# Perceiver block on one core: the value product with two heads' columns as weights, and key blocks in column groups of their own

## Chip, cores and metric
One Trainium2 chip, one core. The metric is the device time of one execution in microseconds, the median over several runs.

## What is computed
A block of three parts, each with a layer norm ahead and a residual: cross attention of 128 rows to a context of 2048 rows, self attention with rotary embedding and a distance bias, and a mixture of 16 experts with the top 4 weighted. Batch 2, width 128, 16 heads of 8. The change touches the cross attention:

```
Qh = _split_heads(Q @ Wq.T + bq)
Kh = _split_heads(K @ Wk.T + bk)
Vh = _split_heads(V @ Wv.T + bv)
scores = jnp.einsum('bhqd,bhkd->bhqk', Qh, Kh) / scale
scores = scores - jnp.max(scores, axis=-1, keepdims=True)
attn = jax.nn.softmax(scores, axis=-1)
attn = jnp.clip(attn, EPS, None)
attn = attn / jnp.sum(attn, axis=-1, keepdims=True)
ctx = jnp.einsum('bhqk,bhkd->bhqd', attn, Vh)
```

## The kernel before
Each engine's program is written out by hand and synchronised with semaphores.

**Ahead.** Keys and values are projected from the context (`keys`, `vals`), keys are split into three bf16 parts whose sum is the fp32 key, and are stacked in `kst` for each pair of heads. The values lie in `vau` as [128 keys, block, head, 9]: eight columns and a column of ones, so that the same product gives the sum of the exponentials.

**The steps.** The cross attention runs in 64 steps (`TILES`), step t for batch t // 32, a group of four heads (t % 32) // 8 and two key blocks of 128. TensorE's order in a step, set by the loop at L1495:
- `scores(t)`, L1252: 8 products, which fill two PSUM banks of [128 keys, 512] (half a has heads a and a + 2 of the group for both blocks). The banks rotate among three (`EBANK`), so a score bank is free when ScalarE's exponential of three jobs before has read it (`bank_free`).
- now and then `turn` (L1233): the row maxima of the next head group are put into the queries' rows, once in eight steps; and small jobs of the first batch's way to the self attention (`SMALL_AT`), among them `sums_out` in step 34.
- `unit(t + 12)`, L1214: queries times keys for the maxima, 1024 columns in two banks, up to step 51. VectorE reduces it (`maxima`, L597).
- `values(t - 1)`, L1271: the value product, below.

ScalarE takes the exponentials (L1030), two of 512 columns per step, into four buffers `ex`. At step 32 it copies the accumulator bank 7 to `oS` (L1042) and `values(32)` waits for that.

**The value product before.** For each block i and head j of the group, weights are the 9 columns of `vau` and the moving operand is 128 columns of exponentials. The output of head j lies at partitions 32j to 32j + 8 of bank 7, so the four heads use four column groups of the array side by side, and a head group has 128 columns of the bank; a batch fills it with its four head groups. All 16 key blocks accumulate in place. In the trace each fp32 product is two hardware passes: 8 products are 16.

**Sums.** `sums_out` turns `oS` with four transposes (`turn_sums`, L1337) into PSUM, [128 queries, 4 groups, 4 heads, 32], of which `sums_in` (L624) and `normalise` (L618, L619) on VectorE read the sums and the values. For batch 0 this is in step 34, for batch 1 at L1585, after the last step: there TensorE's queue goes on with `norms` (L1096), `turn_normed2` (L1444), `sums_out(1)`, `logits_fixed` (L1528, L1529) and the experts' up projections (L1520), whose results ScalarE takes through GELU (L1052), after a table load.

**Beside the path.** GpSimd issues the loads of the constants (L469) and builds the position table `alibi` (L476), between pieces of the maxima (`max_terms`, L413 to L416) for which `turn` waits. The branch `clip_moves`/`clip_sums` is a slow way for rows that need the clip; with these inputs it isn't entered.

Of the kernel before, what the change touches and what calls it, by code (L numbers as in the profile page):

```python
# [25 lines left out]
B, S, D, H = 2, 128, 128, 16  # L26
DK = D // H
# [3 lines left out]
NK = CTX // 128  # L31
PAIRS = H // 2
GH = 4
NG = H // GH
# [16 lines left out]
def build(nc, x, ctxT, wq, wk, wv, wo, bias, bo, qkvw, projw, projb, slopes,  # L51
# [4 lines left out]
    with ExitStack() as es:  # L56
# [3 lines left out]
        def sem(name):  # L60
# [11 lines left out]
        sumrow = sb("sumrow", [128, GH])  # L72
# [30 lines left out]
        oS = sb("oS", [128, B, 512])  # L103
# [22 lines left out]
        fo = sb("fo", [128, 128])  # L126
# [36 lines left out]
        fe, fC = kr[:, 0, 0:512], kr[:, 0, 512:1024]  # L163

# [25 lines left out]
            "oS", "oT", "bnd", "cnt", "flag", "cn", "cnT", "cnTc", "o")}  # L190
# [69 lines left out]
        oS_v = oS[:].rearrange("p b n -> p (b n)")  # L260

# [9 lines left out]
        def clip_moves(sp, b):  # L271

            with sp.Fori(0, NG) as n:
                for r in range(2):
                    for a in range(2):
                        half = slice(HALF * a, HALF * a + HALF)
                        sp.dma_start(fq[half, r, a, :], qst[half, bass.ds(2 * n + r, 1), b * S:(b + 1) * S]
                                     .rearrange("p r n -> p (r n)")).then_inc(d_fg[b], 16)
                sp.dma_start(fo[:], oS[:, b, bass.ds(128 * n, 128)]).then_inc(d_fg[b], 16)
# [6 lines left out]
                sp.dma_start(oS[:, b, bass.ds(128 * n, 128)], facc[:]).then_inc(d_fs[b], 16)  # L286
            sp.wait_ge(d_fs[b], NG * 16)
            sp.wait_ge(f_end[b], 1)
# [223 lines left out]
        def _(dve):  # L512
# [100 lines left out]
            def normalise(b, bank):  # L613

                r = b % B
                o = ps[:, bank, :].rearrange("p (n g c) -> p n g c", n=NG, g=GH)
                r4 = rec[:, r, :].rearrange("p (n g) -> p n g", n=NG)
                link(dve.reciprocal(r4, o[:, :, :, DK]))  # L618
                dve.tensor_tensor(cn[:, r, :].rearrange("p (n g d) -> p n g d", n=NG, g=GH), o[:, :, :, 0:DK],  # L619
                                  r4.unsqueeze(3).broadcast_to([128, NG, GH, DK]), ALU.mult).then_inc(s["cn"], 1)  # L620

            def sums_in(b, bank):
                dve.wait_ge(s["oT"], 2 * b + 1)
                link(dve.tensor_copy(sumq[:, b, :].rearrange("p (n g) -> p n g", n=NG),  # L624
                                     ps[:, bank, :].rearrange("p (n g c) -> p n g c", n=NG, g=GH)[:, :, :, DK]))
# [100 lines left out]
            def normalise2(b):  # L726
                dve.wait_ge(s["oT"], 2 * b + 2)
                normalise(b, SELF[NG * b + 1])
# [10 lines left out]
            def small(kind, bank):  # L739

                if kind == "sums":
                    sums_in(0, bank)
                    normalise(0, bank)
# [86 lines left out]
            normalise(1, SUMS_B)  # L830
# [56 lines left out]
            with dve.If(bad_rows(dve)):  # L887
                dve.wait_ge(d_x, 2 * 16)
                link(dve.tensor_tensor(xs[:], xs[:], boB[:].unsqueeze(1).broadcast_to([128, B, D]), ALU.add))
                for b in range(B, 2 * B):  # L890
# [5 lines left out]
                    normalise(b, SUMS_B)  # L896
# [25 lines left out]
        def _(act):  # L922
# [110 lines left out]
            for t in range(TILES):  # L1033
# [50 lines left out]
        def _(pe):  # L1084
# [174 lines left out]
            def values(t):  # L1259
# [90 lines left out]
            def clip_sums(b):  # L1350
# [3 lines left out]
                with pe.Fori(0, NG) as n:  # L1354
                    pe.wait_ge(d_fg[b], (n + 1) * 80)
                    for j in range(GH):
                        last = pe.matmul(ps[:, CLIP_C, 128 * j:128 * j + 128], sumrow[:, j:j + 1].broadcast_to([128, 128]),
                                         fo[:], start=True, stop=True)
                    last.then_inc(f_C[b], 1)
                    with pe.Fori(0, NK) as c:  # L1360
# [8 lines left out]
                        for j in range(GH):  # L1369
                            last = pe.matmul(ps[32 * j:32 * j + DK + 1, CLIP_PV, 0:128], fv[:, j, :], fe[:, 128 * j:128 * j + 128],  # L1370
# [4 lines left out]
                turn_sums(oS[:, b], SUMS_B).then_inc(f_end[b], 1)  # L1375
# [305 lines left out]

def pick_tables():
# [11 lines left out]
def shape_tables():  # L1694
# [11 lines left out]
    sumrow = np.zeros((128, GH), np.float32)  # L1706
    sumrow[32 * np.arange(GH) + DK, np.arange(GH)] = 1
# [35 lines left out]
```

## Time and profile before

| | us |
|---|---|
| runs before | 215.56, 219.44, 219.81 (median 219.44) |
| the profiled execution | 215.47 |
| its span, first to last instruction | 213.7 |
| TensorE busy in the span | 190.7 (89%) |
| VectorE, ScalarE, GpSimd busy | 146.4, 149.1, 76.0 |
| mean granted TensorE clock | 0.999 of full |

The profile is of one execution. Times of rows are microseconds from the span's start. PE is TensorE's matmul, PEld its weight load, DVE VectorE, ACT ScalarE, POOL GpSimd. An arrow in brackets names what ended the idle time before a row. The steps of the cross attention lie between 39 and 130 us.

### The profile page before, as it was taken

Reading aid. Unit: us, or ns where it says so; the run is one execution under the profiler, and the core shown is the slowest. Engines: PE = TensorE matmul, PEld = TensorE weight load, DVE = VectorE, ACT = ScalarE, POOL = GpSimd, SP = SyncE. Lnnn points to the kernel's source line nnn. Section 1 sums busy time; section 2 is a strip of 40 time slices with the busy share of each in tenths; the row PEclk is TensorE's granted clock in tenths of the full one; section 3 lists DMA queues with packets and bytes.
Section 4 is the critical chain, followed back from the end, with each engine's and each line's share of the span. In section 5 each row is a group of like instructions: output and inputs, shape, how many; then the busy total and the mean of one; then the engine's idle time right before and its main releaser. Section 6 shows DMA issues by size and latency. Waiting matters only on the chain.

```text
span 213.7 us, 6350 instructions
## 1 busy us (share of the span) xinstructions
PE 190.7 (89%) x2551; PEld 131.4 (61%) x2551; DVE 146.4 (69%) x263; ACT 149.1 (70%) x331; POOL 76.0 (36%) x111
## 2 busy tenths in 40 slices
PE   4799899699999989979899999799889999999691
PEld 1345436355555545435454667697769998999681
DVE  5286499999999988988999846746983447212120
ACT  4677684589999988857798972977664645367760
POOL 6123689989889970110200001510000114090000
PEclk9999999999999999999999999999999999999999
DMA  6935332237347322257787712300000000000000
GB/s 115 303 123 216 115 94 92 90 100 272 104 112 200 106 88 83 95 164 213 213 325 231 232 38 77 123 2 0 3 0 3 0 0 15 0 2 3 0 0 25
DMA packets 8690, 21.26 MB, mean 100 GB/s; under 512 B 1664, under 2 KB 2784, under 8 KB 8656
## 3 DMA queue, kind: packets, MB, share of 16 engines
q1 hardware_dynamic: 7344, 19.47, 28.7%
q0 software_dynamic: 592, 0.74, 1.5%
q10 hardware_dynamic: 720, 0.59, 0.8%
q8 instruction: 22, 0.36, 0.7%
q14 instruction: 12, 0.10, 0.1%
HBM read 17.52 MB, written 3.28 MB: 97 GB/s over the span
## 4 chain that ended last, share of the span: by engine, by line
PE 67%; DVE 14%; ACT 8%; issue 3%; DMA 3%; POOL 2%; ACTq 1%; DVEq 0%
PE ps L1271 14%; PE ps L1520 12%; PE ps L1252 10%; PE ps L1553 9%; PE ps L1214 6%; DVE mx L597 5%; PE ps L1119 4%; DMA wks<-in_wk 3%; PE ps L1126 2%; ACT cT L1052 2%; PE ps L1138 2%; PE ps L1411 2%; POOL wr L495 1%; DVE sm L708 1%; ACT ex L1030 1%
## 5 line engine op out<-in xcount | busy, mean ns | idle before, releaser
L597 DVE TENSOR_REDUCE mx<-ps 128x2 f32<-128x1024 f32 x64 | 75.2, 1220 | 7.0 <-PE ps L1214 6.8
L1030 ACT ACTIVATE ex<-ps 128x512 f32<-128x512 f32 x128 | 69.5, 595 | 14.4 <-PE ps L1252 11.3
L1271 PE MATMUL ps<-ex,vau 128*9 128x128 f32 x1024 | 40.0, 274 | 0.5 <-ACT oS L1042 0.4
L1520 PE MATMUL ps<-xT,w1s 128*128 128x128 f32 x256 | 34.4, 278 | 1.5 <-ACT cT L1052 1.3
L1520 PEld LDWEIGHTS ps<-xT,w1s 128*128 128x128 f32 x256 | 31.1, 192 | 2.9 <-ACT cT L1052 2.1
L803 DVE SCALAR_TENSOR_TENSOR xs<-ps,wr,xs 128x128 f32<-128x128 f32 x32 | 11.2, 350 | 31.4 <-PE ps L1553 31.3
L1271 PEld LDWEIGHTS ps<-ex,vau 128*9 128x9 f32 x1024 | 22.0, 90 | 16.1 <-ACT ex L1030 11.7
L1052 ACT ACTIVATE ex<-ps,b1s 128x128 f32<-128x128 f32 x64 | 18.2, 371 | 12.9 <-PE ps L1520 12.7
L1252 PE MATMUL ps<-qst,kst 64*128 64x128 bf16 x512 | 25.5, 217 | 1.3 <-ACT ex L1030 0.9
L1214 PE MATMUL ps<-kst,qst 64*128 64x512 bf16 x128 | 25.1, 380 | 1.6 <-DVE mx L597 1.6
L1252 PEld LDWEIGHTS ps<-qst,kst 64*128 64x128 bf16 x512 | 16.0, 93 | 16.4 <-ACT ex L1030 11.2
L1052 ACT ACTIVATE cT<-ps,b1s 128x128 f32<-128x128 f32 x64 | 18.1, 371 | 10.4 <-PE ps L1520 10.4
L398 POOL TENSOR_TENSOR rstd<-rstd,expo 128x1 f32<-128x1 f32 (+1 forms) x5 | 2.9, 590 | 52.7 <-DVE rstd L529 52.7
L1553 PE MATMUL ps<-kst,cT 128*128 128x128 f32 x128 | 17.4, 279 | 2.2 <-ACT cT L1052 1.7
L1553 PE MATMUL ps<-kst,ex 128*128 128x128 f32 x128 | 17.6, 280 | 0.3 <-ACT ex L1052 0.3
L1553 PEld LDWEIGHTS ps<-kst,cT 128*128 128x128 f32 x128 | 15.5, 192 | 3.5 <-ACT cT L1052 2.6
L1553 PEld LDWEIGHTS ps<-kst,ex 128*128 128x128 f32 x128 | 15.5, 192 | 1.1 <-ACT ex L1052 0.5
L1214 PEld LDWEIGHTS ps<-kst,qst 64*128 64x128 bf16 x128 | 6.7, 93 | 8.6 <-issue 4.4
L1119 PE MATMUL ps<-cT,wks 128*128 128x512 f32 x16 | 10.5, 757 | 0.7 <-DMA wks<-in_wk 0.7
L413 POOL CAST mpad<-mx 128x4 bf16<-128x4 f32 x7 | 1.4, 202 | 25.8 <-DVE mx L603 25.3
L1126 PEld LDWEIGHTS ps<-wvs,cT 128*128 128x128 f32 x64 | 7.8, 191 | 2.7 <-issue 1.8
L495 POOL TENSOR_TENSOR wr<-expo,wr 128x16 f32<-128x16 f32 x2 | 5.8, 2908 | 9.7 <-DVE wr L774 9.7
(207 smaller groups left out, 251.7 us busy)
## 6 DMA issues: line engine op xcount, KB each, us to landing
kst<-parts_d SPq DMA_DIRECT2D x84, 64.0 KB
w1s<-in_w SPq DMA_DIRECT2D x8, 512.0 KB, 4.4
kst<-in_w SPq DMA_DIRECT2D x8, 512.0 KB, 4.6
parts_d<-w1s SPq DMA_DIRECT2D x4, 768.0 KB, 3.7
cT<-in_ctxT SPq DMA_DIRECT2D x3, 512.0 KB, 5.2
cT<-in_ctxT SPq DMA_DIRECT2D x2, 256.0 KB, 5.0
picks<-in_pick ACTq DMA_DIRECT2D x1, 384.0 KB, 5.4
qkvs<-in_qkvw POOLq DMA_DIRECT2D x1, 192.0 KB, 3.4
```

Of the source, the lines that this page charges most:

```text
L495: pool.tensor_tensor(wr[:, b, :], expo[:, 8:8 + E], wr[:, b, :], ALU.pow).then_inc(s["rexd"], 1)
L597: dve.tensor_reduce(out=mx2[:, b, 2 * pair:2 * pair + 2, f], in_=ps[:, bank:bank + 2, :], axis=AX.X, op=ALU.max).then_inc(s["redA"], 1)
L803: dve.scalar_tensor_tensor(out=xs[:, r, :], in0=ps[:, DBANK["down", j], 0:D], scalar=wr[:, r, e:e + 1], in1=xs[:, r, :], op0=ALU.mult, op1 ...
L1030: act.activation(ex[:, e % NE, :], ps[:, EBANK["exp", e], :], ACT.Exp, scale=SCALE).then_inc(s["exp"], 1)
L1052: act.activation(hid[j % N_HID][:, n, :], ps[:, SELF[j % 2], 128 * n:128 * n + 128], ACT.Gelu, bias=b1s[:, FC * e + n:FC * e + n + 1]).the ...
L1119: pe.matmul(ps[:, K_BANK[u], :], wks[:], cTf[:, 512 * u:512 * u + 512], start=True, stop=True)\
L1126: last = pe.matmul(ps[:, bank, 128 * j:128 * j + 128], cTf[:, 128 * c:128 * c + 128], wvs[:], start=True, stop=True)
L1214: last = pe.matmul(ps[:, bank + a, :], qst[half, pair, b * S:(b + 1) * S], kst[half, b, pair, 512 * f:512 * f + 512], start=True, stop=Tru ...
L1252: last[a] = pe.matmul(ps[:, EBANK["exp", 2 * t + a], col:col + 128], kst[half, b, r0 + r, 128 * (c0 + c):128 * (c0 + c) + 128], qst[half, ...
L1271: last = pe.matmul(ps[32 * j:32 * j + DK + 1, 7, 128 * hg:128 * hg + 128], vau[:, NK * b + c, GH * hg + j, :], ex[:, (2 * t + j % 2) % NE, ...
L1520: last = pe.matmul(ps[:, SELF[j % 2], 128 * n:128 * n + 128], w1s[:, f0:f0 + 128], xT[:, (b % B) * S:(b % B + 1) * S], start=True, stop=True)
L1553: last = pe.matmul(ps[:, DBANK["down", j], 0:D], hid[j % N_HID][:, n, :], w2s[:, FC * e + n, :], start=(n == 0), stop=(n == FC - 1))
```

## The change
A value product now has two heads' columns as weights (18) and both heads' exponentials as the moving operand (256 columns). Of its output [18, 256], head r's rows with head r's columns are wanted; the other half is not used. A step has four products: (block i, half a), each in its own column group at partition 32(2i + a). So the two key blocks of a step accumulate in different groups and are added later. A head group takes 256 columns of bank 7; two head groups fill it, and it is copied out after each 16 steps: at steps 16, 32 and 48 by ScalarE, and at the end by VectorE as before. `values` at steps 16, 32 and 48 wait for the copy. The sums are turned by 8 products with the copied sums (128x128) as weights and 18 columns of a table `sumrow`, which picks the wanted rows and adds the two blocks. The second batch's copy lies in `kr`, free by then. The value weights' columns are put in another order on the host.

```diff
-        oS = sb("oS", [128, B, 512])
+        oS0 = sb("oS0", [128, 1024])
...
+        oS = [oS0[:], kr[:, 1, :]]
...
-                if t == TILES // 2:
-                    act.wait_ge(s["pv"], TILES // 2)
-                    act.activation(oS[:, 0, :], ps[:, 7, :], ACT.Copy).then_inc(s["oS"], 1)
+                if t and t % 16 == 0:
+                    act.wait_ge(s["pv"], t)
+                    b, h0 = (t - 16) // 32, 512 * ((t // 16 - 1) % 2)
+                    act.activation(oS[b][:, h0:h0 + 512], ps[:, 7, :], ACT.Copy).then_inc(s["oS" if h0 else "oSh"], 1)
...
                 if t == TILES // 2:
                     pe.wait_ge(s["oS"], 1)
+                elif t and t % 16 == 0:
+                    pe.wait_ge(s["oSh"], t // 32 + 1)
                 for i in range(2):
                     c = 2 * (t % 8) + i
-                    for j in range(GH):
-                        last = pe.matmul(ps[32 * j:32 * j + DK + 1, 7, 128 * hg:128 * hg + 128],
-                                         vau[:, NK * b + c, GH * hg + j, :],
-                                         ex[:, (2 * t + j % 2) % NE, 128 * (2 * i + j // 2):128 * (2 * i + j // 2) + 128],
-                                         start=(c == 0), stop=(c == NK - 1), tile_position=(0, 32 * j))
+                    for a in range(2):
+                        q = 32 * (2 * i + a)
+                        last = pe.matmul(ps[q:q + 2 * (DK + 1), 7, 256 * (hg % 2):256 * (hg % 2) + 256],
+                                         vau[:, NK * b + c, GH * hg + 2 * a:GH * hg + 2 * a + 2, :].rearrange("p h d -> p (h d)"),
+                                         ex[:, (2 * t + a) % NE, 256 * i:256 * i + 256],
+                                         start=(t % 8 == 0), stop=(t % 8 == 7), tile_position=(0, q))
                 last.then_inc(s["pv"], 1)
...
             def sums_out(b, bank):
                 pe.wait_ge(s["oS"], 2 * b + 1)
+                pe.wait_ge(d_const, 16 * N_CONST)
                 if b:
                     pe.wait_ge(s["exp"], 2 * TILES)
-                turn_sums(oS[:, b], bank).then_inc(s["oT"], 1)
+                for h in range(H // 2):
+                    last = pe.matmul(ps[:, bank, 2 * (DK + 1) * h:2 * (DK + 1) * (h + 1)], oS[b][:, 128 * h:128 * h + 128],
+                                     sumrow[:, GH + 2 * (DK + 1) * (h % 2):GH + 2 * (DK + 1) * (h % 2 + 1)], start=True, stop=True)
+                last.then_inc(s["oT"], 1)
...
-            dve.tensor_copy(oS[:, 1, :], ps[:, 7, :]).then_inc(s["oS"], 1)
+            dve.tensor_copy(oS[1][:, 512:1024], ps[:, 7, :]).then_inc(s["oS"], 1)
...
-        "wq": i[p + "Wq"][ROWS].T, "wk": i[p + "Wk"][ROWS].T, "wv": i[p + "Wv"].T, "wo": i[p + "Wo"].T,
+        "wq": i[p + "Wq"][ROWS].T, "wk": i[p + "Wk"][ROWS].T, "wv": i[p + "Wv"][VCOLS].T, "wo": i[p + "Wo"].T,
```

How TensorE's order stands around `sums_out(0)`, step 34, before:

```order
L1252 MATMUL ps<-qst,kst 128x128 x8
L1214 MATMUL ps<-kst,qst 128x512 x2
L1271 MATMUL ps<-ex,vau 9x128 x8
L1252 MATMUL ps<-qst,kst 128x128 x8
L1337 MATMUL ps<-ident,oS 128x128 x4
L1214 MATMUL ps<-kst,qst 128x512 x2
L1271 MATMUL ps<-ex,vau 9x128 x8
```

and now, with the same places (scores, keys' product, values, scores, sums, keys' product, values):

```order
L1258 MATMUL ps<-qst,kst 128x128 x8
L1220 MATMUL ps<-kst,qst 128x512 x2
L1280 MATMUL ps<-ex,vau 18x256 x4
L1258 MATMUL ps<-qst,kst 128x128 x8
L1355 MATMUL ps<-sumrow,oS 128x18 x8
L1220 MATMUL ps<-kst,qst 128x512 x2
L1280 MATMUL ps<-ex,vau 18x256 x4
```

Nothing moves; the value product's 8 short products are 4 long ones, and the 4 transposes are 8 products of 18 columns at the same place.

Two pieces of ScalarE's order before, from before step 16 and around step 32 (`ex` exponentials, `qst` the maxima's rows, `oS` the copy):

```order
L1030 ACTIVATE ex<-ps 128x512 [waits s_pv,s_scB] x16
L1019 ACTIVATE qst<-ps 3x2x128 [waits s_mT]
L1019 ACTIVATE qst<-ps 3x2x128
L1030 ACTIVATE ex<-ps 128x512 [waits s_pv,s_scB] x16
...
L1030 ACTIVATE ex<-ps 128x512 [waits s_pv,s_scB] x4
L1042 ACTIVATE oS<-ps 128x512 [waits s_pv]
L1030 ACTIVATE ex<-ps 128x512 [waits s_pv,s_scB] x12
```

and the same two places now, and that of step 48:

```order
L1035 ACTIVATE ex<-ps 128x512 [waits s_pv,s_scB] x4
L1048 ACTIVATE oS<-ps 128x512 [waits s_pv]
L1035 ACTIVATE ex<-ps 128x512 [waits s_pv,s_scB] x12
...
L1035 ACTIVATE ex<-ps 128x512 [waits s_pv,s_scB] x4
L1048 ACTIVATE oS<-ps 128x512 [waits s_pv]
L1035 ACTIVATE ex<-ps 128x512 [waits s_pv,s_scB] x12
...
L1048 ACTIVATE kr<-ps 128x512 [waits s_pv]
L1035 ACTIVATE ex<-ps 128x512 [waits s_pv,s_scB] x10
```

A copy stands after the exponentials of steps 16 and 48 too, the last of them into `kr`.

## Rows read from the trace of the kernel before

**Rows 1.** Page, chain that ended last, shares of the span by engine
```profile
PE 67%; DVE 14%; ACT 8%; issue 3%; DMA 3%; POOL 2%; ACTq 1%; DVEq 0%
```

**Rows 2.** Page, costliest groups: busy us, mean ns, idle before and its releaser
```profile
L597 DVE TENSOR_REDUCE mx<-ps 128x2 f32<-128x1024 f32 x64 | 75.2, 1220 | 7.0 <-PE ps L1214 6.8
L1030 ACT ACTIVATE ex<-ps 128x512 f32<-128x512 f32 x128 | 69.5, 595 | 14.4 <-PE ps L1252 11.3
L1271 PE MATMUL ps<-ex,vau 128*9 128x128 f32 x1024 | 40.0, 274 | 0.5 <-ACT oS L1042 0.4
```

**Rows 3.** Timeline of steady steps (start, us, engine line, what, idle before)
```profile
50.78 4.70 DVE L597 TENSOR_REDUCE mx<-ps 128x2 f32<-128x1024 f32 x4
51.70 5.24 ACT L1030 ACTIVATE ex<-ps 128x512 f32<-128x512 f32 x9
...
52.99 0.34 PEld L1271 LDWEIGHTS ps<-ex,vau 128*9 128x9 f32 x16 [0.26 <-ACT ex L1030]
...
53.60 0.40 PE L1252 MATMUL ps<-qst,kst 64*128 64x128 bf16 x8
...
54.15 0.34 PEld L1271 LDWEIGHTS ps<-ex,vau 128*9 128x9 f32 x16 [0.26 <-ACT ex L1030]
...
54.73 0.26 PEld L1252 LDWEIGHTS ps<-qst,kst 64*128 64x128 bf16 x8 [0.25 <-ACT ex L1030]
```

**Rows 4.** Timeline of steps 32 to 35, with the copy and the sums
```profile
80.61 0.34 PEld L1271 LDWEIGHTS ps<-ex,vau 128*9 128x9 f32 x16 [0.26 <-ACT ex L1030]
...
81.45 0.60 ACT L1042 ACTIVATE oS<-ps 128x512 f32<-128x512 f32 x1
...
82.17 0.37 PEld L1271 LDWEIGHTS ps<-ex,vau 128*9 128x9 f32 x16 [0.67 <-ACT ex L1030]
...
83.08 0.42 PEld L1337 LDWEIGHTS ps<-ident,oS 128*128 128x128 f32 x4
...
83.67 0.10 PEld L1214 LDWEIGHTS ps<-kst,qst 64*128 64x128 bf16 x2 [0.17 <-issue]
...
83.78 0.17 DVE L624 COPY sumq<-ps 128x16 f32<-128x16 f32 x1 [0.68 <-PE ps L1337]
...
84.00 0.34 PEld L1271 LDWEIGHTS ps<-ex,vau 128*9 128x9 f32 x16 [0.23 <-ACT ex L1030]
...
84.55 0.22 PEld L1252 LDWEIGHTS ps<-qst,kst 64*128 64x128 bf16 x8 [0.22 <-ACT ex L1030]
```

**Rows 5.** Passes by line: duration min/median/max in ns
```profile
L1119 PE MATMUL ps<-cT,wks x16: 592/697/1220, 7.2 to 29.8; 128*128 128x512 f32 x16
...
L1271 PE MATMUL ps<-ex,vau x1024: 270/273/278, 41.9 to 129.8; 128*9 128x128 f32 x171
```

**Rows 6.** Timeline: turns of the maxima in steps 14 and 30, and GpSimd
```profile
57.05 0.26 PEld L1252 LDWEIGHTS ps<-qst,kst 64*128 64x128 bf16 x8 [0.25 <-ACT ex L1030]
57.54 0.13 PEld L1233 LDWEIGHTS ps<-identb,mpad 128*128 128x128 bf16 x2 [0.23 <-issue]
...
73.03 3.61 POOL L476 TENSOR_TENSOR alibi<-dist,sl 128x2048 f32<-128x2048 f32 x1
...
76.76 0.26 PEld L1252 LDWEIGHTS ps<-qst,kst 64*128 64x128 bf16 x8 [0.25 <-ACT ex L1030]
77.79 0.11 PEld L1233 LDWEIGHTS ps<-identb,mpad 128*128 128x128 bf16 x2 [0.78 <-POOL mpad L416]
```

**Rows 7.** Timeline of the bounds' products, 128x128 fp32 weights, 16 moving columns
```profile
183.32 0.30 PEld L1109 LDWEIGHTS ps<-blocks,qsq 128*128 128x128 f32 x2
...
183.99 0.30 PEld L1111 LDWEIGHTS ps<-blbk,qf 128*128 128x128 f32 x2
```

**Rows 8.** Timeline after the last step: the second batch's sums
```profile
131.44 0.42 PEld L1337 LDWEIGHTS ps<-ident,oS 128*128 128x128 f32 x4 [0.46 <-DVE oS L827]
...
131.83 0.30 PEld L1528 LDWEIGHTS ps<-ksq,neg 128*128 128x128 f32 x2
...
133.72 1.28 ACT L1052 ACT_TABLE_LOAD   x1 [4.33 <-PE ps L1520]
```

More of the change, by code:

```diff
@@ L71, in build @@
         quart = sb("quart", [128, GH])
-        sumrow = sb("sumrow", [128, GH])
+        sumrow = sb("sumrow", [128, GH + 4 * (DK + 1)])
         xs = sb("xs", [128, B, D])
@@ L125, in build @@
         fv = sb("fv", [128, GH, DK + 1])
-        fo = sb("fo", [128, 128])
         facc = sb("facc", [128, 128])
@@ L163, in build @@
         fe, fC = kr[:, 0, 0:512], kr[:, 0, 512:1024]
+        oS = [oS0[:], kr[:, 1, :]]
+        fo = qr[:].rearrange("p (r n) -> p r n", r=2)
         kp = w1s[:, 0:6144].bitcast(bf16).rearrange("p (n t k) -> p n t k", n=2 * B, t=3)
@@ L611, in maxima, with head_sums, turned_sums, normalise @@
                     dve.tensor_tensor(m[:, :, 2], mxr[:], m[:, :, 1], ALU.subtract).then_inc(s["mpad"], 1)
-            def normalise(b, bank):
+            def head_sums(bank):
+                return ps[:, bank, 0:H * (DK + 1)].rearrange("p (n g c) -> p n g c", n=NG, g=GH)
+            def turned_sums(bank):
+                return ps[:, bank, :].rearrange("p (n g c) -> p n g c", n=NG, g=GH)
+            def normalise(b, o):
                 r = b % B
-                o = ps[:, bank, :].rearrange("p (n g c) -> p n g c", n=NG, g=GH)
                 r4 = rec[:, r, :].rearrange("p (n g) -> p n g", n=NG)
@@ L624, in sums_in @@
                 link(dve.tensor_copy(sumq[:, b, :].rearrange("p (n g) -> p n g", n=NG),
-                                     ps[:, bank, :].rearrange("p (n g c) -> p n g c", n=NG, g=GH)[:, :, :, DK]))
+                                     head_sums(bank)[:, :, :, DK]))
             def lowest():
@@ L727, in normalise2 @@
                 dve.wait_ge(s["oT"], 2 * b + 2)
-                normalise(b, SELF[NG * b + 1])
+                normalise(b, turned_sums(SELF[NG * b + 1]))
             def sums2(b):
@@ L742, in small @@
                     sums_in(0, bank)
-                    normalise(0, bank)
+                    normalise(0, head_sums(bank))
                 if kind == "heads":
@@ L895, in _ @@
                     clip_sums(r)
-                    normalise(b, SUMS_B)
+                    normalise(b, turned_sums(SUMS_B))
                     heads_turned(b, HEADS_B)
@@ L1357, in clip_sums @@
                         last = pe.matmul(ps[:, CLIP_C, 128 * j:128 * j + 128], sumrow[:, j:j + 1].broadcast_to([128, 128]),
-                                         fo[:], start=True, stop=True)
+                                         fo[:, j // 2, :], start=True, stop=True)
                     last.then_inc(f_C[b], 1)
@@ L1369, in clip_sums @@
                         for j in range(GH):
-                            last = pe.matmul(ps[32 * j:32 * j + DK + 1, CLIP_PV, 0:128], fv[:, j, :], fe[:, 128 * j:128 * j + 128],
+                            last = pe.matmul(ps[32 * j:32 * j + DK + 1, CLIP_PV, 0:128], fv[:, 2 * (j % 2) + j // 2, :], fe[:, 128 * j:128 * j + 128],
                                              start=True, stop=True, tile_position=(0, 32 * j))
@@ L1374, in clip_sums @@
                 pe.wait_ge(d_fs[b], NG * 16)
-                turn_sums(oS[:, b], SUMS_B).then_inc(f_end[b], 1)
+                turn_sums(oS[b], SUMS_B).then_inc(f_end[b], 1)
             def turn_heads(b, bank):
@@ L1679 @@
 ROWS = np.arange(D).reshape(2, 4, 2, DK).transpose(1, 0, 2, 3).reshape(D)
+VCOLS = np.arange(D).reshape(NG, 2, 2, DK).transpose(0, 2, 1, 3).reshape(D)
 def pick_tables():
@@ L1705, in shape_tables @@
     quart = np.tile(np.repeat(np.eye(GH, dtype=np.float32), DK, axis=0), (NG, 1))
-    sumrow = np.zeros((128, GH), np.float32)
-    sumrow[32 * np.arange(GH) + DK, np.arange(GH)] = 1
+    n9 = DK + 1
+    sumrow = np.zeros((128, GH + 4 * n9), np.float32)
+    for i in range(2):
+        for a in range(2):
+            for r in range(2):
+                p0 = 32 * (2 * i + a) + n9 * r
+                sumrow[p0 + DK, 2 * r + a] = 1
+                sumrow[p0 + np.arange(n9), GH + 2 * n9 * r + n9 * a + np.arange(n9)] = 1
     return {"ident": ident, "blocks": blocks, "rot": rot, "dist": dist, "tri": tri, "quart": quart, "sumrow": sumrow, "pick": pick_tables()}
```

9 lines of the change are left out of this document (4 added, 5 removed).

## Prediction

> **What bounds the kernel now.** I read the page first, then the costliest groups, then the timeline of one steady step, then the timeline at each place that the diff touches. The page says that two thirds of the chain that ended last lie on TensorE [rows 1]. That tempts one to price the change by the TensorE time of the value product, 40.0 us in 1024 hardware passes, which is 16 passes and 0.62 us for each of the 64 steps [rows 2]. The same group list warns that the key maxima on VectorE (64 of 1220 ns) and the exponentials on ScalarE (128 of 595 ns) are of the same size per step [rows 2].
>
> The timeline of a steady step decides it [rows 3]. The weight loads of the value product begin at 52.99 in one step and at 54.15 in the next, so a step takes 1.16 us. VectorE works without a gap (4.70 us for four maxima, 1.17 each), ScalarE nearly so (5.24 us for nine exponentials). And TensorE waits each time before the scores: their weight loads are released by an exponential, after 0.25 us of idle load time [rows 3]. That is a closed loop of latencies: a score bank is free only when an exponential of the step before has read it, so the scores wait for that, and the next exponential waits for the scores. Of the 1.16 us the exponential takes 0.595 [rows 2], the scores 0.40 [rows 3], and the rest, 0.165, is left for the two signals between the engines and the first load. The value product is not in this loop; it stands in TensorE's queue between two turns of it. How much room it has there is read from a step in which TensorE was late: from the first value load to the next score load it needs 0.55 us (84.00 to 84.55) [rows 4], and in the steady step 0.58 pass (54.15 to 54.73) [rows 3]. So a shorter product gains nothing in a steady step, and one longer by over 0.03 us begins to cost.
>
> **The value product.** Before, each of the four column groups of the array does two products of 128 columns per step, in two passes each: four passes of 128 columns. Now each does one product of 256 columns, in two passes. The columns that a group streams are the same 512, because half of each result (one head's values with the other head's exponentials) is thrown away. What a pass costs beyond its columns comes from two rows: a pass of 512 columns takes 592 ns at least, one of 128 takes 273 in the middle [rows 5], so 384 columns cost 319 ns, 0.83 ns each, and about 167 ns are a tail that overlaps with the next pass. A pass of 256 takes 273 + 106 = 379. Four rounds of about 107 become two of about 213, the start offsets of the four groups (under 0.03 us in all) stay, and the last pass ends 0.62 us after the first load, as before. I take -0.01 us where TensorE is late (some 12 steps: those from 52 to 63, beside the self attention of the first batch, and a few after stalls), together -0.1, and 0 elsewhere. The bounds: if the price were one per instruction, 0.62/16 = 0.039 us each [rows 2], eight fewer would save 0.31 per step where TensorE is late. If instead four long streams don't run side by side as well as the short ones, nothing in this trace excludes a few tenths more per step; no row shows 256-column passes of this kind in four groups.
>
> The row speaks against a rule of the Trainium skill here, which is the rule that would argue for this change. The page TensorEngine Tiling (Array Packing), section Instruction Overhead, says that each matmul carries about 60 cycles of overhead. By it, an estimate, two passes fewer in each group are 120 cycles of 2.4 GHz, 50 ns per step and 3.2 us over 64 steps if all of them were on the path; by the rows it is hidden in the tail and the steady loop hides what is left.
>
> **Two more bank copies on ScalarE.** A head group now takes 256 columns of the accumulator bank, so the bank is full after 16 steps and is copied out at steps 16, 32 and 48 by ScalarE (before: 32 only) and at the end by VectorE, as before. The trace has the price at step 32: the copy stands behind the two exponentials, takes 0.60 us, and the next value product waits for it: from 80.61 to 82.17 is 1.56 us where a step has 1.16 [rows 3, 4]; its first load stands idle for 0.67 us before it, in a steady step for 0.26. So 0.40 us each. At step 48 nothing later waits for a thing of fixed time, and I count +0.40. At step 16 the cost ends in an existing wait: at step 30 the turning of the maxima waits for GpSimd, which is late with the position table (3.61 us from 73.03) that stands ahead of it in its queue [rows 6]. In step 14 that load follows the score load by 0.49 us (57.05, 57.54), in step 30 by 1.03 (76.76, 77.79), and its idle time of 0.78 is put down to GpSimd [rows 6]. The 0.54 us in between swallow 0.40. So 0 (upper bound 0.40).
>
> **The sums turned.** Before, 4 transposes of 128 columns turn the sums. Now 8 products with the sums (128x128, fp32) as weights and 18 moving columns both turn and pick. Each is two passes with a weight load of 128 fp32 columns. The trace has this form: the bounds' products (128x128 fp32 weights, 16 moving columns) have their loads at 183.32 and, three products later, at 183.99: 0.67/3 = 0.223 us each, 0.112 per load [rows 7]. They are bound by the load, however few columns move. 8 x 0.223 = 1.79 us.
> First batch, step 34: the transposes begin at 83.08 and the next loads of the keys' product at 83.67 [rows 4]; 0.42 of that is loading and the rest is draining. Now 1.79 and a little over 0.1 of draining: +1.3. TensorE is late there already (its next score load follows the values by 0.55, not 0.58 [rows 4]), and VectorE waits for the same sums (0.68 us) before it can take the next maxima [rows 4], so both move together. +1.3 us.
> Second batch: transposes begin at 131.44, the next product's load at 131.83, 0.39 us [rows 8]; now 1.79: +1.4. Behind it in TensorE's queue stand the first two up projections; ScalarE's table load waits for the first of them at 133.72 [rows 8], and everything after it follows in chain. +1.4 us. The bound from below for each is 0, if the path ran elsewhere; from above some 0.2 more, what a last load and the draining can leave in view.
>
> **Edits at nothing.** The wait for the constants before the sums: the position table, which is made from them, begins at 73.03 [rows 6], before step 34. The constant table with 40 columns for 4: 18 KB more in a transfer that nothing waits for. The reciprocal and the scaling read the same 16 and 128 elements at another stride; I take 0 for it, and no row prices it. The order of value weights is changed on the host. The clip path isn't run.
>
> **The sum.** 215.47 (the profiled execution: span 213.7 and 1.8 around it) - 0.1 + 0 + 0.4 + 1.3 + 1.4 = 218.5 us. That is +1.4%. A measurement of this kernel tells about 2% from no change, so this is "within 2%". The profiled execution stands at the low end of the runs before (215.56, 219.44, 219.81); the median lies 3.97 above it. If the changed kernel's median falls like that, the same +3.0 reads 222.5; the range has to hold this too.
>
> **Rivals.**
> A. *The value product is priced by instruction.* For it: 16 short passes per step, all with a load of their own. Against: the passes of one group are spaced like their columns, and the loop of rows 3. Where TensorE is late, from step 52 on and after stalls, at most some 24 steps x 0.31 = -7.4: 215.47 + 3.1 - 7.4 = 211.2.
> B. *Slower by over 2%: the long streams run worse side by side.* Place: every step. For it: no row shows it, and the room is only 0.03 us. Price at 0.1 us more per step: 64 x (0.10 - 0.03) = 4.5, so 223.0. It decides from +0.05 per step (64 x 0.02 = 1.3 on top of 3.0 is 2%). Against: columns per group, offsets and bank are the same.
> C. *The first sums' cost is taken up later*, as that of step 16 is: VectorE and TensorE wait for each other in steps 36 to 47 around the first batch's normalisation. Against: every one of those waits begins with the sums themselves. Then 217.2.
>
> **How the numbers follow.** Forecast 0.68, A 0.06, B 0.16, C 0.10. The range from 216.0 holds C and the forecast, and its upper end of 223.5 holds B and the forecast on the median's level; left out are A and the far part of B. Faster by over 2% is most of A, 0.05; slower by over 2% is B, 0.16; within 2% is the rest, 0.79.
>
> **What would show it.** In the profile after: a steady step still of 1.16 us and value loads to score loads near 0.58; 512 passes of near 379 ns with nearly the same busy time, 40 us; ScalarE's copy three times, with steps of 1.56 at 16, 32 and 48; at step 30 the wait for GpSimd shrunk by 0.4, and the time there as before; the sums' products 1.8 us wide, twice, and the table load later by 3.0 than at 133.72. The prediction is wrong if the steady step differs from 1.16 in either direction, or if the busy time of the value product leaves 36 to 44 us.

## The result, and the profile after

| | runs, us | median |
|---|---|---|
| before, beside the change | 215.56, 219.44, 219.81, 215.69 | 217.56 |
| changed | 219.63, 221.71, 221.64, 220.49 | 221.06 |
| before, later, 13 runs on the chip of `g1_after_again` | 215.24 to 219.0 | 215.50 |
| changed, again, 4 runs there | 220.64 to 221.04 | 220.84 |

The changed kernel is slower. The ratio was 1.0243 (95%: 1.0147 to 1.034) at first and 1.0237 (1.0213 to 1.0261) when it was run again beside 13 runs of before; there the medians lie 5.3 us apart. The forecast was 218.5 us, 3.0 over the profiled execution of before; the profiled execution of after took 219.63, with a span of 217.8. The ratios leave out runs more than 1.5% above the fastest of their kernel, such as 219.44 and 219.81 of before, of which only one like them came in 34 later runs (219.0, with a mean clock of 0.98).

The costliest groups of the changed kernel, for the lines of [rows 2]:

```profile
L597 DVE TENSOR_REDUCE mx<-ps 128x2 f32<-128x1024 f32 x64 | 75.4, 1220 | 8.0 <-PE ps L1220 7.8
L1035 ACT ACTIVATE ex<-ps 128x512 f32<-128x512 f32 x128 | 69.5, 596 | 15.7 <-PE ps L1258 12.9
L1280 PE MATMUL ps<-ex,vau 128*18 128x256 f32 x512 | 40.1, 385 | 1.3 <-ACT oS L1048 0.7
```

Half the passes, 40.1 us for 40.0. By line, the pass itself:

```profile
L1280 PE MATMUL ps<-ex,vau x512: 376/379/393, 41.8 to 131.9; 128*18 128x256 f32 x171
```

379 ns in the middle, as worked out from 273 and 592. (The profile models the ends of passes, so their starts and those of the loads are the firmer evidence.) Twelve steps near the end, where TensorE is the late one, take 18.78 us from value load to value load (112.03 to 130.81), and took 18.79 before (109.85 to 128.64): half the passes gained 0.01 us there. A steady step in the timeline, for [rows 3]:

```profile
52.88 0.13 PEld L1280 LDWEIGHTS ps<-ex,vau 128*18 128x18 f32 x8 [0.27 <-ACT ex L1035]
...
54.05 0.13 PEld L1280 LDWEIGHTS ps<-ex,vau 128*18 128x18 f32 x8 [0.27 <-ACT ex L1035]
...
54.63 0.25 PEld L1258 LDWEIGHTS ps<-qst,kst 64*128 64x128 bf16 x8 [0.45 <-ACT ex L1035]
```

A step is 1.16 us within 0.01, and from values to scores is 0.58, both as before. The idle load time before the scores has grown from 0.25 to 0.45, since eight loads fewer are done there, but the load starts when it did: it waits for the exponential. That is what "not in the loop" looks like.

The copies at steps 16 and 48 (weight loads of the value product before and behind):

```profile
60.42 0.14 PEld L1280 LDWEIGHTS ps<-ex,vau 128*18 128x18 f32 x8 [0.26 <-ACT ex L1035]
...
61.98 0.16 PEld L1280 LDWEIGHTS ps<-ex,vau 128*18 128x18 f32 x8 [0.67 <-ACT ex L1035]
...
108.16 0.13 PEld L1280 LDWEIGHTS ps<-ex,vau 128*18 128x18 f32 x8 [0.26 <-ACT ex L1035]
...
109.72 0.16 PEld L1280 LDWEIGHTS ps<-ex,vau 128*18 128x18 f32 x8 [0.67 <-ACT ex L1035]
```

1.56 us each, as at step 32 in [rows 4] and at step 32 here (81.08 to 82.64). Step 30 and GpSimd, for [rows 6]:

```profile
73.14 0.27 POOL L475 TENSOR_SCALAR sl<-slB 128x16 f32<-128x16 f32 x1 [0.64 <-DMA rb_s<-in_rb]
73.49 3.61 POOL L476 TENSOR_TENSOR alibi<-dist,sl 128x2048 f32<-128x2048 f32 x1
...
77.04 0.25 PEld L1258 LDWEIGHTS ps<-qst,kst 64*128 64x128 bf16 x8 [0.45 <-ACT ex L1035]
78.26 0.11 PEld L1239 LDWEIGHTS ps<-identb,mpad 128*128 128x128 bf16 x2 [0.97 <-POOL mpad L416]
```

Scores of step 30 come 0.28 us later than before (the whole attention began 0.1 earlier), so the delay of the copy is there; the turn waits for GpSimd all the same, and GpSimd is itself 0.46 late, for it waited 0.64 us for the last constant to land, where before it went on without that wait.

The first batch's sums, for [rows 4]:

```profile
83.56 1.86 PEld L1355 LDWEIGHTS ps<-sumrow,oS 128*128 128x128 f32 x16
...
85.45 0.10 PEld L1220 LDWEIGHTS ps<-kst,qst 64*128 64x128 bf16 x2
85.56 0.17 DVE L629 COPY sumq<-ps 128x16 f32<-128x16 f32 x1 [1.99 <-PE ps L1355]
```

From the first load to the next product's load 1.89 us for 0.59: +1.30. The second batch's, for [rows 8]:

```profile
133.61 1.86 PEld L1355 LDWEIGHTS ps<-sumrow,kr 128*128 128x128 f32 x16 [0.46 <-DVE kr L832]
...
135.39 0.30 PEld L1541 LDWEIGHTS ps<-ksq,neg 128*128 128x128 f32 x2
...
136.04 1.87 PE L1533 MATMUL ps<-xT,w1s 128*128 128x128 f32 x8
...
138.00 1.28 ACT L1058 ACT_TABLE_LOAD   x1 [6.43 <-PE ps L1533]
```

1.78 us for 0.39: +1.39. Up to 135.39 everything adds up: that load is 3.56 us later than the same one in [rows 8], which is 0.47 at step 30 counted from before's clock time, 1.30, 0.40 and 1.39. But the table load is 4.28 later, and the up projection that it waits for takes 1.87 us here, where it is 1.16 long before (8 passes of 128 columns, at 132.48). The table of stretches tells why (columns: busy time of PE, PEld, DVE, ACT, POOL, granted clock, DMA share, GB/s):

```profile
130.00:136.00 6.00, 5.55 (x83) 4.16 (x79) 2.42 (x9) 1.49 (x3) 0.56 (x1) 1.00 0.30 89
136.00:140.00 4.00, 4.00 (x21) 3.79 (x20) 1.49 (x7) 1.99 (x4) 0.95 (x1) 0.57 0.35 135
140.00:144.00 4.00, 3.46 (x29) 3.21 (x29) 3.60 (x13) 3.73 (x14) 2.34 (x2) 1.00 0.00 0
```

In 136 to 140 the granted clock is 0.57 in the mean, that is the level of 1.2 GHz for most of it. At half the full clock that makes 3.4 of the 4 us. The profiled execution of before has 1.00 from 128 to 142. The forecast had no term for this.

### The profile page after: what moved, and what is told of

The parts are those of the page before. It is cut to its first block, busy times and chain, and to the rows that moved or that the text cites. A ratio compares the mean times of both kernels' runs of the same rounds, so it can differ in the third digit from the quotient of the medians.

```text
span 217.8 us, 5377 instructions
## 1 busy us (share of the span) xinstructions
PE 194.2 (89%) x2062; PEld 122.6 (56%) x2063; DVE 146.5 (67%) x263; ACT 150.1 (69%) x333; POOL 76.0 (35%) x111
## 4 chain that ended last, share of the span: by engine, by line
PE 63%; DVE 16%; ACT 9%; issue 4%; POOL 3%; DMA 2%; ACTq 1%; DVEq 0%; POOLq 0%
PE ps L1533 12%; PE ps L1280 11%; PE ps L1566 9%; PE ps L1258 8%; DVE mx L597 7%; PE ps L1220 5%; PE ps L1125 4%; DMA wks<-in_wk 2%; PE ps L1132 2%; ACT cT L1058 2%; PE ps L1355 2%; PE ps L1144 1%; PE ps L1424 1%; POOL wr L495 1%; ACT ex L1035 1%
## 5 line engine op out<-in xcount | busy, mean ns | idle before, releaser
L1280 PE MATMUL ps<-ex,vau 128*18 128x256 f32 x512 | 40.1, 385 | 1.3 <-ACT oS L1048 0.7
L1533 PE MATMUL ps<-xT,w1s 128*128 128x128 f32 x256 | 35.9, 286 | 0.5 <-ACT cT L1058 0.4
L1533 PEld LDWEIGHTS ps<-xT,w1s 128*128 128x128 f32 x256 | 32.6, 199 | 2.0 <-ACT cT L1058 1.2
L1280 PEld LDWEIGHTS ps<-ex,vau 128*18 128x18 f32 x512 | 9.0, 96 | 17.1 <-ACT ex L1035 12.5
L1125 PE MATMUL ps<-cT,wks 128*128 128x512 f32 x16 | 10.2, 736 | 0.6 <-DMA wks<-in_wk 0.6
```

The lines of the kernel that those rows point to most:

```text
L1125: pe.matmul(ps[:, K_BANK[u], :], wks[:], cTf[:, 512 * u:512 * u + 512], start=True, stop=True)\
L1280: last = pe.matmul(ps[q:q + 2 * (DK + 1), 7, 256 * (hg % 2):256 * (hg % 2) + 256], vau[:, NK * b + c, GH * hg + 2 * a:GH * hg + 2 * a + 2, ...
L1533: last = pe.matmul(ps[:, SELF[j % 2], 128 * n:128 * n + 128], w1s[:, f0:f0 + 128], xT[:, (b % B) * S:(b % B + 1) * S], start=True, stop=True)
```

## The experiments

T1 is the theory of the prediction: the sums cost 2.7 us, the copies 0.4, the value product nothing. After the result came the question of the rest, 0.7 us in the profiled execution and about 2 in the others: the clock, and what brings it down. "Clock" below is the mean granted TensorE clock of an execution, as a share of full. The median of before in each group was: first four 215.95 (13 runs), the `f` four 215.63 (8), the `g` four 215.50 (13).

**The value product in short passes (`e1b_split`).**

```diff
-                        last = pe.matmul(ps[q:q + 2 * (DK + 1), 7, 256 * (hg % 2):256 * (hg % 2) + 256],
-                                         vau[:, NK * b + c, GH * hg + 2 * a:GH * hg + 2 * a + 2, :].rearrange("p h d -> p (h d)"),
-                                         ex[:, (2 * t + a) % NE, 256 * i:256 * i + 256],
-                                         start=(t % 8 == 0), stop=(t % 8 == 7), tile_position=(0, q))
+                        for k in range(2):
+                            c0 = 256 * (hg % 2) + 128 * k
+                            last = pe.matmul(ps[q:q + 2 * (DK + 1), 7, c0:c0 + 128],
+                                             vau[:, NK * b + c, GH * hg + 2 * a:GH * hg + 2 * a + 2, :].rearrange("p h d -> p (h d)"),
+                                             ex[:, (2 * t + a) % NE, 256 * i + 128 * k:256 * i + 128 * k + 128],
+                                             start=(t % 8 == 0 and k == 0), stop=(t % 8 == 7 and k == 1), tile_position=(0, q))
```

> Changed kernel with each value product of 256 columns split into two of 128 (18 weights columns, same column group), so 16 passes and 16 weight loads per step as before the change. Theory T1 (columns count, not instructions; the steady step is a loop of exponential and scores): steady step stays 1.16 us, value loads to score loads 0.58, span within 0.2 us of the changed kernel's 217.8 where the granted clock is the same. Rival A (price per instruction): steps in which TensorE is late grow, span 219 or more. Rival B (long passes run worse side by side): span falls by over 1 us.

Measured: median 223.1 (222.27 to 225.92), 1.0316 of before (1.0288 to 1.0344); the clock was 0.969 to 0.979 in all four. The steady step is 1.16 us, against rival B. The span of 221.7 is over rival A's 219, and not at the changed kernel's clock: in its profile the level fell twice, behind the first sums (0.65 in the mean from 84 to 88, 3.4 us long) and behind the second (from 136.4 on, 10.2 us long). This run alone can't tell the price of the passes from the clock's; it was repeated beside the changed kernel, below.

**The sums' products in the kernel before (`e2_before_products`).** Added work, its results overwritten.

```diff
+                for h in range(H // 2):
+                    pe.matmul(ps[:, bank, 18 * h:18 * h + 18], oS[:, b, 128 * (h % 4):128 * (h % 4) + 128],
+                              ident[:, 0:18], start=True, stop=True)
                 turn_sums(oS[:, b], bank).then_inc(s["oT"], 1)
```

> Kernel before, with 8 products of 128x128 fp32 weights and 18 moving columns added ahead of the four transposes of each batch's sums (their results are overwritten). T1: the two places grow by 1.8 us each, and the span by 3.6 from 213.7, to 217.3, plus 0.5 to 1 us if such a stretch makes the granted clock fall behind the second one. Rival C (the first one is taken up later): 215.5. If the clock drop of the changed kernel's profile (3.4 us at half speed from 136.3) comes from these stretches it appears here within 3 us behind the second; if it is chance, it is not tied to that place.

Measured: 222.28 (220.89 to 223.19), 1.029 of before (1.0238 to 1.0342), so +6.3 us for 3.6 us of products. The clock of the four was 0.974, 0.988, 0.973 and 0.992. Its stretches show where:

```profile
130.00:134.00 4.00, 3.55 (x81) 2.62 (x74) 2.06 (x7) 1.22 (x3) 0.56 (x1) 1.00 0.14 14
134.00:145.00 11.00, 10.78 (x53) 10.30 (x53) 4.25 (x15) 3.86 (x11) 2.91 (x1) 0.53 0.25 92
```

The second stretch of products begins at 133.34, and from 134 to 145 the mean clock is 0.53 (half speed for 10.2 us). No value product was touched here. The drop began within it rather than behind it, against the expectation; that it is bound to that place, and to the sums' products without the rest of the change, is as expected. What the first stretch costs by itself is in `f3_first_only`.

**The same products with 128 streamed columns, in the changed kernel (`e3_wide`).** The table gets zero columns behind; each product overwrites what the one before it wrote too far.

```diff
-                    last = pe.matmul(ps[:, bank, 2 * (DK + 1) * h:2 * (DK + 1) * (h + 1)], oS[b][:, 128 * h:128 * h + 128],
-                                     sumrow[:, GH + 2 * (DK + 1) * (h % 2):GH + 2 * (DK + 1) * (h % 2 + 1)], start=True, stop=True)
+                    last = pe.matmul(ps[:, bank, 2 * (DK + 1) * h:2 * (DK + 1) * h + 128], oS[b][:, 128 * h:128 * h + 128],
+                                     sumrow[:, GH + 2 * (DK + 1) * (h % 2):GH + 2 * (DK + 1) * (h % 2) + 128], start=True, stop=True)
```

> Changed kernel whose sums' products stream 128 columns in place of 18 (the other 110 zero, overwritten by the next product), under the same weight loads. T1 with the clock drop caused by the few columns streamed: the stretches stay 1.8 to 1.9 us, no drop behind them, span 217.3 and the median 1 to 2 us under the changed kernel's. If the drop is chance or comes from elsewhere: no difference to the changed kernel in span or mean clock.

Measured: 219.86 (218.85 to 223.35), 1.0164 of before (1.0132 to 1.0195); clocks 0.995, 0.999, 0.999, 0.999. Seven times the streamed columns, and no fall: the profile has 1.00 from 39 to 200. The median is 1.2 us under the changed kernel's 221.06, which was taken on another occasion; the pair on one chip is below. At step 30 it was late, since GpSimd waited 1.53 us for the constants' landing and began its table at 74.52, where the changed kernel had 73.49. One of the four runs, 223.35, was high at a clock of 0.999; what took the time in it no profile shows.

**The copies alone (`e4_before_copies`).** A copy of bank 7 at steps 16 and 48 of the kernel before, into a tile that nothing reads, and the value products wait for it.

```diff
+                if t in (16, 48):
+                    act.wait_ge(s["pv"], t)
+                    act.activation(junk[:], ps[:, 7, :], ACT.Copy).then_inc(s["oSh"], 1)
...
+                elif t and t % 16 == 0:
+                    pe.wait_ge(s["oSh"], t // 32 + 1)
```

> Kernel before, with bank copies on ScalarE added at steps 16 and 48 and the value product of these steps waiting for them, as in the change. T1: steps 17 and 49 grow by 0.40 each; that of step 16 is swallowed by the wait for GpSimd at step 30 (step 31 starts no later than before unless GpSimd itself is late), so +0.4: span 214.1. If nothing is swallowed: +0.8, 214.5.

Measured: 215.88 over 10 runs, ratio 1.0008 (0.9979 to 1.0037). The span of the profiled one is 214.1, 0.4 over the profiled execution of before, and the table load comes at 134.25, 0.53 later than in [rows 8]. Step 30, in which GpSimd is on time:

```profile
77.03 0.26 PEld L1256 LDWEIGHTS ps<-qst,kst 64*128 64x128 bf16 x8 [0.25 <-ACT ex L1031]
77.69 0.11 PEld L1237 LDWEIGHTS ps<-identb,mpad 128*128 128x128 bf16 x2 [0.41 <-POOL mpad L417]
```

The wait for GpSimd is 0.41 where [rows 6] have 0.78: the copy's 0.40 vanished in it, as forecast. Only the trace shows this; the times don't show the 0.4 us of the other copy (215.88 against 215.95), and their interval of 0.3% either way can't exclude it.

**The added products streaming 128 columns, in the kernel before (`f1_before_wide`).**

```diff
-                    pe.matmul(ps[:, bank, 18 * h:18 * h + 18], oS[:, b, 128 * (h % 4):128 * (h % 4) + 128],
-                              ident[:, 0:18], start=True, stop=True)
+                    pe.matmul(ps[:, bank, 18 * h:18 * h + 128], oS[:, b, 128 * (h % 4):128 * (h % 4) + 128],
+                              ident[:], start=True, stop=True)
```

> Kernel before, with the same 8 added products per batch as in e2_before_products, but each streams 128 columns (all of the identity) under the same weight loads. If the clock falls because the array streams few columns for 1.8 us: the two places cost the same 3.6 us, the mean clock is that of the kernel before (0.99 and more), the median is near 219.5 and 2 to 3 us under that of e2_before_products (222.28). If it falls for any stretch of this length, or by what the weight loads draw: same clock and median as e2_before_products.

Measured: 219.67, 219.93, 222.94, 223.01, with clocks of 0.999, 0.999, 0.994 and 1.000. The clock is as expected in all four, and two runs are at the forecast of 219.5. The other two are 3.2 us over those with hardly any loss of clock, so the median is 221.44, 1.0261 of before (1.0172 to 1.0351), and the forecast of the time was missed. By the time alone this version can't be told from `e2_before_products`; by the clock it can. There is a second effect, seen here twice, in `e3_wide` once and perhaps in `e1b_split` once (225.92 at 0.979, over 222.27 to 223.5), whose place is unknown: each kernel's profile caught an execution without it.

**One stretch at a time (`f2_second_only`, `f3_first_only`).** The edit of `e2_before_products`, with `H // 2 if b == 1 else 0` products, and with `b == 0`.

> Kernel before, with the 8 products of 18 columns added for the second batch alone. If the second stretch, which follows 32 products of 16 columns (the norms), is the one that brings the clock down: +1.8 us of products and +1.5 to 2.7 of clock, 219.3 to 220.4, half speed beginning within 3 us behind it. If each stretch costs only its length: 217.8.

> Kernel before, with the 8 products of 18 columns added for the first batch alone (step 34). Expected +1.8 us, 217.8, and a half-speed stretch behind it in some executions only (the changed kernel's profile shows none there, its split version one of 3.4 us). Rival C (taken up later): 216.

Measured: second only 217.88 (217.54 to 218.25), 1.0097 (1.008 to 1.0114), clocks 0.985 to 0.996; first only 218.33 (217.45 to 218.7), 1.0119 (1.0087 to 1.015), clocks 0.992, 0.999, 0.987, 0.987. Each costs its 1.8 us and 0.4 to 0.9 more, less than expected for the second. The profile of the second only has half speed for 3.4 us, beginning at 134.6, 1.2 us behind the added products. `f3_first_only` answers rival C, by which the first stretch is taken up later: up to the second batch's sums its trace is 1.65 us late (133.09 for 131.44 in [rows 8]), so most of the 1.8 stays. And a surprise in the profile of the first only, whose products stand at step 34: there the clock stays up (1.00 from 39 to 134), and falls at the other place, for 3.4 us from 134.3, where this kernel doesn't differ from before but for being 1.65 us later.

```profile
128.00:134.00 6.00, 5.55 (x124) 3.94 (x116) 3.00 (x12) 2.52 (x5) 0.56 (x1) 1.00 0.12 13
134.00:138.00 4.00, 4.00 (x21) 3.87 (x20) 1.66 (x7) 1.86 (x4) 0.82 (x1) 0.57 0.63 247
```

So the fall at the place behind the last step (32 products of 16 columns, a lone transpose, a wait for VectorE, the sums, the up projections) does not need anything added there. What the first stretch has to do with it is not shown: it may be the shift alone. Together with `e2_before_products` the two don't add up: 2.3 and 2.7 us alone, 6.3 together.

**The wide version with its zeros written on chip (`f4_wide_memset`).** As `e3_wide`, with the zero columns set by GpSimd at the start and only 40 columns transferred, as in the changed kernel.

> Changed kernel with products of 128 columns for the sums as in e3_wide, but the added zero columns written on chip, so that the table's transfer is as long as in the changed kernel. If e3_wide's late position table (73.49 in the changed kernel, 74.52 in e3_wide) came from the longer transfer: its start is back at 72.7 to 73.5 and the time is 0.7 us under e3_wide, near 219.0, mean clock 0.999. If the lateness is that of the load's landing by chance: no difference to e3_wide.

Measured: 218.93 (218.54 to 219.45), clocks 0.994 to 1.000. That is 0.9 us under `e3_wide`, but GpSimd waited again, 1.05 us, and began the table at about 73.6. The lateness comes and goes: the tables begin at 73.49 in the changed kernel, 73.12 in its split version with the same transfer, 73.57 in `f1_before_wide` with the transfer of before. Over all profiles with the table in its old place in the queue, GpSimd waited for the last constant in five of five with 8 passes per step (0.20 to 1.53 us) and in one of eight with 16 (0.42). No run tests what is behind this, and what decides how late the last constant lands stays open.

**The pairs on one chip (`g1_after_again`, `g2_split_again`, `g4_wide_again`).** The unedited changed kernel, the split one and that of `f4_wide_memset`.

> The changed kernel, unedited, beside the others on one chip. If the theory's terms (sums 2.7, copy 0.4, late position table 0 to 0.5, clock 0.5 to 2) are complete: median 219.5 to 221, mean clock under 0.992 in most executions, steady step 1.16.

> The split version of e1b_split again, beside the changed kernel on the same chip. If the number of passes has a price of its own only through the clock: mean clock lower than the changed kernel's (0.97 to 0.98) and median 1 to 3 us over it. If e1b_split's low clock was chance or the other chip's: same median within 0.5 us.

> The version of f4_wide_memset again, beside the changed kernel on the same chip. If few streamed columns in the sums bring the clock down: mean clock 0.995 and more, median 1 to 2 us under the changed kernel. If not: no difference.

| | median, us | range | clock of the four runs |
|---|---|---|---|
| changed | 220.84 | 220.64 to 221.04 | 0.980 to 0.981 |
| split into 128 columns | 221.81 | 220.88 to 221.88 | 0.974 to 0.978 |
| changed, sums streaming 128 columns | 218.88 | 218.6 to 219.09 | 0.999 to 1.000 |

The changed kernel and the wide one don't overlap: 1.96 us, with the same instructions in the same places but for the streamed columns of 16 products and one write of zeros on GpSimd at the start (`e3_wide`, without that write, kept its clock too). The same stretches of the two, the changed kernel first:

```profile
130.00:134.00 4.00, 3.55 (x66) 2.22 (x64) 2.06 (x7) 1.40 (x3) 0.56 (x1) 1.00 0.01 2
134.00:136.00 2.00, 2.00 (x18) 1.97 (x17) 0.43 (x2) 0.00 (x0) 0.00 (x0) 0.91 0.91 274
136.00:142.00 6.00, 5.78 (x26) 5.34 (x26) 2.76 (x10) 3.46 (x9) 2.62 (x1) 0.50 0.21 86
142.00:144.00 2.00, 1.88 (x16) 1.69 (x14) 1.77 (x7) 1.21 (x5) 0.28 (x1) 0.88 0.00 0
```

```profile
130.00:134.00 4.00, 3.55 (x68) 2.02 (x61) 2.12 (x8) 1.67 (x4) 0.56 (x1) 1.00 0.01 2
134.00:136.00 2.00, 2.00 (x19) 1.97 (x18) 0.12 (x1) 0.00 (x0) 0.00 (x0) 1.00 0.82 229
136.00:142.00 6.00, 4.66 (x39) 4.39 (x39) 4.55 (x16) 4.31 (x13) 2.91 (x1) 1.00 0.25 101
```

In the six microseconds from 136 on, 26 passes are done at 1.2 GHz, and 39 at 2.4 GHz although TensorE waits more. And the first up projection and the third, the changed kernel's pair first:

```profile
136.16 2.08 PE L1533 MATMUL ps<-xT,w1s 128*128 128x128 f32 x8
...
140.81 1.94 PE L1533 MATMUL ps<-xT,w1s 128*128 128x128 f32 x8 [0.22 <-ACT cT L1058]
```

```profile
136.22 1.16 PE L1534 MATMUL ps<-xT,w1s 128*128 128x128 f32 x8
...
139.95 1.16 PE L1534 MATMUL ps<-xT,w1s 128*128 128x128 f32 x8 [1.34 <-ACT cT L1059]
```

The third waits 1.34 us for ScalarE where the clock is full and 0.22 where it is half, so part of the half-speed time is hidden in the wait for the table load and the GELUs. By the clock column the half-speed part is 6.8 us long (0.4 before 136, 6 from 136 to 142, 0.5 behind). If TensorE were the limit all through it, half of that would be lost, 3.4 us; the wait takes up 1.1 (1.34 for 0.22), an estimate of 2.3 is left, and about 2 are measured. The rows place these 2 us. The load behind the second sums (131.83 before) begins 3.47 us later in the changed kernel (135.30) and 3.74 later in the wide one; at the end of the span the changed kernel is 5.5 us longer than before (219.2 for 213.7), the wide one 3.6 (217.3). So all of the difference comes behind the sums, where the one runs at half speed and the other doesn't.

The length of the half-speed part differs between executions of one kernel: 3.4 us in the first profile of the changed kernel and 6.8 in this one. In the first, half of it is 1.7, of which the third up projection's wait took up 0.9 (0.43 us for 1.34); that fits with the 0.7 that it cost.

The split version is 0.97 us over the changed one, with a lower clock again (half speed for 10.2 us in its profile), and its steady step is 1.16. The doubled passes take little by themselves: in the 12 late steps the value loads lie 18.87 us apart (111.62 to 130.49), 0.1 more than with half the passes. The rest goes with the clock; why it stays down longer here is open.

**A try at a faster version (`g3_before_pool_order`).** In the kernel before, GpSimd's piece for step 30 goes ahead of its position table.

```diff
+            max_terms(4)
             link(pool.tensor_scalar(sl8[:], slB[:], MAX_BIAS, None, ALU.mult))
             link(pool.tensor_tensor(alibi[:], dist[:].unsqueeze(1).broadcast_to([128, H, 128]),
                                     sl8[:].unsqueeze(2).broadcast_to([128, H, 128]), ALU.mult))
-            max_terms(4)
```

> Kernel before, GpSimd's piece of the maxima for step 30 moved ahead of the position table. The wait of step 30 (0.54 us over that of step 14) was the slack that the copy of step 16 vanished in. If it lies on the path: step 31 starts 0.5 us earlier and the span is 213.2, 0.2% under before. If something else is due there: no difference.

```profile
76.40 0.22 POOL L416 TENSOR_TENSOR mpad<-mxr,mpad 128x4 bf16<-128x4 f32 x1
...
77.06 3.61 POOL L477 TENSOR_TENSOR alibi<-dist,sl 128x2048 f32<-128x2048 f32 x1
```

```profile
76.81 0.25 PEld L1252 LDWEIGHTS ps<-qst,kst 64*128 64x128 bf16 x8 [0.25 <-ACT ex L1030]
77.30 0.13 PEld L1233 LDWEIGHTS ps<-identb,mpad 128*128 128x128 bf16 x2 [0.23 <-issue]
```

The turn follows the scores by 0.49 us, as in step 14, and the span is 213.4. Median 215.08 against 215.50, ratio 0.998 (0.9958 to 1.0001): near the forecast in size, and not told from no change.

## Why the prediction was right and wrong

- **What bounds the kernel: right.** The steady step is 1.16 us in every version that was looked at, with 8 or 16 passes. Rival A (price per instruction) falls: in the 12 late steps, where it would be paid, half the passes gained 0.01 us and splitting them again cost 0.1. The forecast's own -0.1 for these steps was not there either. Rival B (long passes side by side run worse) falls: 379 ns per pass and 0.58 us from values to scores, as worked out.
- **The sums turned: right.** Forecast +1.3 and +1.4, measured +1.30 and +1.39. Rival C falls: in the changed kernel the first +1.30 is still there at the load behind the second sums, and in `f3_first_only` 1.65 of the added 1.8.
- **The copies: right.** 0.40 each, and that of step 16 vanished in the wait for GpSimd, shown in `e4_before_copies`. The bound of 0 for step 16 left out that GpSimd can itself be late. "A transfer that nothing waits for" was read wrongly: GpSimd waits for all the constants ahead of its position table. It was 0.46 us late in the profiled execution and 0.37 in the repeated one (73.40); whether the longer table has a part in it is open.
- **The clock: the step that failed.** The term "The sums turned" priced the products by their length alone, and took what follows them at the full clock. The products stream 18 columns under loads of 128 for 1.8 us, soon after 32 products of 16 columns, and behind the second ones the granted clock falls to 1.2 GHz: for 6.8 us in the profiled one of the repeated executions, whose clock of 0.981 the other three share (0.980, 0.981, 0.981). It costs 0.7 us in the first profiled execution (table load 4.28 later where 3.56 is explained) and 2.0 in the median of the repeated run (220.84 against 218.88 with 128 streamed columns). In the span of the repeated profile the terms are 3.1 as forecast, 0.4 for the late constants and 2.0 for the clock, together the 5.5 us by which it is longer than before's. That the streamed columns decide it in the changed kernel is shown by this pair; how they do so, and why the fall also came in `f3_first_only` with no product added at that place, is open.
- **The level and the sign.** 218.5 is above the profiled execution and below the median of 219.44 shown then. As a time beside that median it reads as no change or a little faster, though the sum said +1.4%. Two of the three times shown were high ones, of a kind seen once in 34 later runs. That the upper end of the range holds the result is in part luck. Stated as a difference the forecast was +3.0 us; measured +5.3. "Within 2%" had 0.79; the ratio of 1.024 lies over it. The range of 216.0 to 223.5 holds 221.06, for its upper end had been set for a higher level and for rival B, not for the clock.

## What to carry to other kernels

Joining small products into one with a half that is thrown away saved instructions here, not columns; count what each column group streams, and look for the loop that sets the step before crediting anything. Where an output layout saves work in the loop, price what undoes the layout: here 16 loads of 128 fp32 columns for 18 columns each. And price such load-bound products twice, by their length and by what they do to the granted clock of what follows; streaming columns of zeros under the loads cost nothing in length (1.86 us of loads either way) and gave 2 us back in this kernel, though the kernel before stays the faster one.

## What the runs showed of the hardware that was not expected

- The granted clock fell to 1.2 GHz while TensorE was counted busy for all of the two microseconds in which it fell (2.00 of 2.00 from 134 to 136), and in the four before its longest wait was 0.27 us, for VectorE. The Trainium skill's page TensorE: Matmul & The Clock Gate, section "HAM oscillation — how this bites in real kernels", tells of a fall in gaps in which TensorE waits for DMA. This trace has no such gap ahead of the fall. What the two kernels differ in is how many columns move: the same loads with 128 streamed columns kept the level in 8 of 8 runs (clock 0.994 and more), with 18 the clock was 0.981 or less in four of four.
- A kernel with products added at step 34 alone had its clock fall 50 us later, in a place of which nothing was changed (`f3_first_only`: the profiled execution, and by clocks of 0.987 two of the other three). Why is open.
- The part at half speed was 3.4 us in one execution of the changed kernel and 6.8 in another, and cost 0.7 and 2.0 us, less than half its length, where TensorE's wait for ScalarE shrank from 1.34 us to 0.43 and 0.22.
- Three runs of versions that stream 128 columns there (`e3_wide` once, `f1_before_wide` twice) took 3 to 4 us more than the others of their kernel at a clock of 0.994 and more. No profile caught one, and the cause is open.
